# Second feed-forward: TensorE signals twice per pass, at a greater distance between up and down

## The reference

```python
x = x + jnp.tanh(g_ffn[1]) * _L1_ffn_ref(_layernorm(x, axis=-1), ...)

topk_idx, topk_weight = _gate(x, gate_w, e_bias)      # 4 of 16 experts for each row
g = jnp.einsum('th,eih->eti', x, gate_proj)           # 256 -> 128
u = jnp.einsum('th,eih->eti', x, up_proj)             # 256 -> 128
inter = jax.nn.silu(g) * u
expert_out = jnp.einsum('eti,ehi->eth', inter, down_proj)   # 128 -> 256
sel = expert_out[topk_idx, jnp.arange(T)[:, None]]
y = jnp.einsum('tkh,tk->th', sel, topk_weight)
shared_out = jax.nn.silu(sg) * su @ shared_down_w.T
return y + shared_out
```

## Time and profile before

| | |
|---|---|
| median of three runs | 1418.01 us (1416.52 to 1421.49) |
| span of the profiled execution, the only time of its own that the page gives | 1481.7 us |
| busy over the span: TensorE (matmul) | 1190.4 us, 80% |
| VectorE | 911.7 us, 62% |
| ScalarE | 784.9 us, 53% |
| GpSimd | 516.5 us, 35% |

### The profile page before, as it was taken

How to read it: one execution, slowest core, us unless ns; L and a number is a source line. 1 busy time by engine, 2 the same in 40 slices (tenths; PEclk the granted TensorE clock), 3 DMA queues, 4 the chain that set the end, 5 groups by cost and what they waited for, 6 DMA issues and landing times. The chain is left out here.

```text
span 1481.7 us, 27979 instructions
## 1 busy us (share of the span) xinstructions
PE 1190.4 (80%) x9258; PEld 1081.2 (73%) x9258; DVE 911.7 (62%) x2119; ACT 784.9 (53%) x2205; POOL 516.5 (35%) x585
## 2 busy tenths in 40 slices
PE   2776249997899999999999999975898767778674
PEld 1555139887799998888888888875887766667563
DVE  3887645552666666678657787766876322234667
ACT  2776115552566667665657665554654433345442
POOL 3566033553000001100354005543634555654442
PEclk9676559998999999999999999997999878889897
DMA  7753224553722000100233003443844545444896
GB/s 139 206 173 125 81 84 136 153 151 76 199 65 66 8 2 22 30 8 2 69 112 107 16 3 128 129 146 112 285 125 144 154 150 154 150 129 147 284 285 224
DMA packets 139588, 177.13 MB, mean 120 GB/s; under 512 B 22048, under 2 KB 120512, under 8 KB 139456
## 3 DMA queue, kind: packets, MB, share of 16 engines
q1 hardware_dynamic: 110752, 122.57, 28.8%
q0 software_dynamic: 17792, 43.14, 9.0%
q10 hardware_dynamic: 10912, 9.70, 1.9%
HBM read 107.28 MB, written 68.09 MB: 118 GB/s over the span
## 5 line engine op out<-in xcount | busy, mean ns | idle before, releaser
L1690 ACT ACTIVATE attend_s<-attend_s,attend_less 128x128 f32<-128x128 f32 x512 | 198.3, 392 | 108.4 <-DVE attend_less L1831 99.9
L2331 POOL DMA_INDIRECT answers<-ahead_plain,moe_dst x160 | 157.4, 984 | 186.5 <-ACT ahead_plain L2410 97.5
L1643 POOL TENSOR_TENSOR router_xn<-rest_acc,router_mv 128x512 f32<-128x512 f32 x12 | 12.7, 1058 | 426.6 <-DVE router_rs L1294 372.3
L81 PE MATMUL moe_psU<-moe_wh,moe_xl 128*128 (+1 forms) x384 | 118.1, 308 | 4.3 <-issue 3.3
L2477 DVE TENSOR_TENSOR moe_it<-moe_it,moe_psU 128x256 f32<-128x256 f32 x96 | 40.2, 418 | 128.9 <-ACT moe_it L2392 82.6
L83 PE MATMUL moe_psU<-moe_wh,moe_xh 128*128 (+1 forms) x384 | 115.9, 302 | 3.3 <-issue 3.2
L82 PE MATMUL moe_psU<-moe_wl,moe_xh 128*128 (+1 forms) x384 | 116.5, 303 | 2.3 <-issue 2.2
L1262 POOL DMA_INDIRECT slots<-router_row,router_idx x80 | 81.0, 1013 | 93.9 <-DMA router_row<-normed_rows 62.2
L1708 ACT ACTIVATE attend_pt<-attend_psS 128x1024 f32<-128x1024 f32 x64 | 65.5, 1024 | 83.2 <-PE attend_psS L1982 82.0
L1829 DVE SCALAR_TENSOR_TENSOR attend_s<-attend_psS,held_bias 128x1024 f32<-128x1024 f32 x64 | 78.0, 1219 | 44.3 <-PE attend_psS L1975 44.2
L2640 PE MATMUL moe_psI<-const_ident,moe_it 128*128 128x128 f32 x192 | 42.1, 305 | 78.4 <-DVE moe_il L2473 68.0
(11 more groups left out here) (384 smaller groups left out, 4175.6 us busy)
## 6 DMA issues: line engine op xcount, KB each, us to landing
ahead_plain<-slots SPq DMA_DIRECT2D x160, 129.0 KB
moe_both<-answers SPq DMA_DIRECT2D x28, 512.0 KB
router_row<-normed_rows SPq DMA_DIRECT2D x40, 256.0 KB
layer_raw<-in_wi_dram SPq DMA_DIRECT2D x8, 1024.0 KB, 4.8
layer_raw<-in_wo_dram SPq DMA_DIRECT2D x8, 1024.0 KB, 6.8
slots<-router_xn SPq DMA_DIRECT2D x4, 2048.0 KB, 11.0
ahead_plain<-in_gex_dram SPq DMA_DIRECT2D x17, 384.0 KB
moe_both<-normed_rows SPq DMA_DIRECT2D x24, 256.0 KB
```

The costliest lines, as they stand in the source:

```text
L81: pe.matmul(out, wl, mh, start=first, stop=False)
L1690: last = nc.scalar.activation(s[:, g, j, :], s[:, g, j, :], ACT.Exp, bias=less[:, g, j:j + 1], accum_out=sm[:, g, j:j + 1])
L2331: nc.gpsimd.indirect_dma_start(out=R.YT[q], out_offset=bass.IndirectOffsetOnAxis(ap=dst[:, r % NM, s:s + 1], axis=0), in_=yb[:, r % NY, s, ...
```

## The change

TensorE's four signals per pass become two. `upped` is raised by the last matmul of up(j), which now follows turn(j+2) and stands for both. `passed` is raised at the end of a pass, by turn_inner(j-2), which now follows down(j-4), and stands for both. All waits on the old four are put in terms of these. The table read stands at the end of the pass. There are 100 passes instead of 98, `it` has three buffers instead of two, the routing weights and targets twelve instead of eight, and the copy of the weights moves from ScalarE (`weighted`, removed with its semaphore) to VectorE's `targets`. The answers are asked for two passes later.

```diff
-    NT, NS, NM = 2, 4, 8
+    NT, NS, NM = 2, 4, 12
+    TURN_AHEAD, INNER_BEHIND, DOWN_BEHIND = 2, 2, 4
+    PASSES = PAIRS_ALL + DOWN_BEHIND
-        it = sb("it", [P, 2, 2, I1])
+        it = sb("it", [P, 3, 2, I1])
+        def pass_over(eng, j):
+            eng.wait_ge(passed, j - INNER_BEHIND + 1)
+        def turn_done(eng, j):
+            eng.wait_ge(upped, j + 1)
+        def up_done(eng, j):
+            eng.wait_ge(upped, j + TURN_AHEAD + 1)
+        def inner_done(eng, j):
+            pass_over(eng, j + INNER_BEHIND)
+        def down_done(eng, j):
+            pass_over(eng, j + DOWN_BEHIND)
-        answered_from = STARTS_OF[1] + NX + 4
+        answered_from = STARTS_OF[1] + NX + 4 + DOWN_BEHIND - 2
@@ SyncE, load
-                    sp.wait_ge(t_done, j - NX + 1)
+                    turn_done(sp, j - NX)
                     if not is_shared(j - NX):
                         sp.wait_ge(d_up, NTH[j - NX] + 1)
-                        sp.wait_ge(g_up, NTH[j - NX] + 1)
@@ ScalarE
-            for j in range(PAIRS_ALL + 2):
+            for j in range(PASSES):
+                if j + TURN_AHEAD < PAIRS_ALL:
+                    x_high(j + TURN_AHEAD)
                 if j < PAIRS_ALL:
                     silu(j)
-                if j + 2 < PAIRS_ALL:
-                    x_high(j + 2)
-                    if not is_shared(j + 2):
-                        weighted(j + 2)
-                if 1 <= j <= PAIRS_ALL:
-                    i_high(j - 1)
-                if j >= 2 and not is_shared(j - 2):
-                    y_out(j - 2)
+                if 0 <= j - INNER_BEHIND < PAIRS_ALL:
+                    i_high(j - INNER_BEHIND)
+                if j >= DOWN_BEHIND and not is_shared(j - DOWN_BEHIND):
+                    y_out(j - DOWN_BEHIND)
@@ VectorE, targets
+                v.tensor_copy(wd[:, r % NM, :], xg[:, j % NX, :, D])
@@ VectorE (its loop: x_low(j+2), inner(j), i_low(j-2), targets(j+2), add(j-4))
@@ TensorE
-            for j in range(PAIRS_ALL + 2):
+            for j in range(PASSES):
+                if j + TURN_AHEAD < PAIRS_ALL:
+                    last = turn(j + TURN_AHEAD)
                 if j < PAIRS_ALL:
-                    up(j, bases[j])
+                    last = up(j, bases[j])
+                    last.then_inc(upped, 1)
+                if j >= DOWN_BEHIND:
+                    last = down(j - DOWN_BEHIND, bases.pop(j - DOWN_BEHIND))
+                if 0 <= j - INNER_BEHIND < PAIRS_ALL:
+                    last = turn_inner(j - INNER_BEHIND)
+                if j >= INNER_BEHIND:
+                    last.then_inc(passed, 1)
                 if j + 1 in STARTS_OF:
                     pe.wait_ge(table_up, KIND[j + 1] + 1)
                 if j + 1 < PAIRS_ALL:
                     bases[j + 1] = bases_of(j + 1)
-                if j + 2 < PAIRS_ALL:
-                    turn(j + 2)
-                if 1 <= j <= PAIRS_ALL:
-                    turn_inner(j - 1)
-                if j >= 2:
-                    down(j - 2, bases.pop(j - 2))
```

More of the change, by code:

```diff
@@ L2382, in x_high @@
             def x_high(j):
-                act.wait_ge(t_done, j + 1)
+                turn_done(act, j)
                 nc.scalar.activation(xh[:, j % 2, :], psX[j % 2][:], ACT.Copy).then_inc(x_hi, 1)
             def i_high(j):
-                act.wait_ge(i_done, j + 1)
+                inner_done(act, j)
                 nc.scalar.activation(ih[:, j % 2], psI[:, 0:N], ACT.Copy).then_inc(i_hi, 1)
             def silu(j):
[L2391 to L2400, removed]
+                up_done(act, j)
+                nc.scalar.activation(it[:, j % 3], psU[j % 2][:].rearrange("p (s n) -> p s n", s=2)[:, :, 0:I1], ACT.Silu).then_inc(s_up, 1)
             def y_out(j):
                 r = NTH[j]
-                act.wait_ge(y_done, j + 1)
-                act.wait_ge(g_up, r + 1)
+                down_done(act, j)
+                act.wait_ge(d_up, r + 1)
                 if r >= NY:
@@ L2476, in inner @@
                 dve.wait_ge(s_up, j + 1)
[L2477 removed]
+                v.tensor_tensor(it[:, j % 3], it[:, j % 3], psU[j % 2][:].rearrange("p (s n) -> p s n", s=2)[:, :, I1:2 * I1], ALU.mult).then_inc(i_up, 1)
             def add(j):
[L2481 removed]
+                down_done(dve, j)
                 a = rows(acc[:, 2 * NTH[j]:2 * NTH[j] + 2, :])
@@ L2555, in _ @@
             R.aggregate(dve, LAST, stat3)
-            for j in range(PAIRS_ALL + 2):
+            for j in range(PASSES):
+                if j + TURN_AHEAD < PAIRS_ALL:
+                    x_low(j + TURN_AHEAD)
                 if j < PAIRS_ALL:
                     inner(j)
-                if j + 2 < PAIRS_ALL:
-                    x_low(j + 2)
-                if 1 <= j <= PAIRS_ALL:
[L2562 to L2566, removed]
+                if 0 <= j - INNER_BEHIND < PAIRS_ALL:
+                    i_low(j - INNER_BEHIND)
+                if j + TURN_AHEAD < PAIRS_ALL and not is_shared(j + TURN_AHEAD):
+                    targets(j + TURN_AHEAD)
+                if j >= DOWN_BEHIND and is_shared(j - DOWN_BEHIND):
+                    add(j - DOWN_BEHIND)
                 for k in (2 * j + 1, 2 * j + 2):
@@ L2609, in turn @@
                         last = nc.tensor.transpose(psX[j % 2][:, k * N + s * P:k * N + (s + 1) * P], xg[:, j % NX, s, k * P:(k + 1) * P], C["ident"][:])
-                last.then_inc(t_done, 1)
+                return last
             def bases_of(j):
@@ L2632, in up @@
                                        [part(w, bases[s], k * 2 * I1, 2 * I1) for w in (wh, wl)], k == 0, k == KD - 1)
-                last.then_inc(u_done, 1)
+                return last
             def turn_inner(j):
@@ L2639, in turn_inner @@
                 for s in range(2):
-                    last = nc.tensor.transpose(psI[:, s * P:(s + 1) * P], it[:, j % 2, s, :], C["ident"][:])
-                last.then_inc(i_done, 1)
+                    last = nc.tensor.transpose(psI[:, s * P:(s + 1) * P], it[:, j % 3, s, :], C["ident"][:])
+                return last
             def down(j, bases):
@@ L2650, in down @@
                                    [part(w, bases[s], 4 * I1, D) for w in (wh, wl)], True, True)
-                last.then_inc(y_done, 1)
+                return last
             split(pe, 0)
-            turn(0)
-            turn(1)
+            turn(0).then_inc(upped, 1)
+            turn(1).then_inc(upped, 1)
             bases = {0: bases_of(0)}
-            for j in range(PAIRS_ALL + 2):
+            for j in range(PASSES):
                 if j == STARTS_OF[0]:
```

8 lines of the change are left out of this document (4 added, 4 removed).

## The result

The changed kernel takes 1431.07 us (median of four runs, 1428.84 to 1432.39), the kernel before 1418.59 beside it (four runs). The ratio is 1.0081, 95% interval 1.0056 to 1.0106: slower by 12.5 us. The forecast was 1424.6, slower, with a range of its own of 1419 to 1430.

What follows compares the result with a forecast made beforehand. No engine was taken as full; TensorE's 2.79 us was the floor of a pass. 5.6 - 0.4 + 0.8 + 0.6 = +6.6 us on 1418.0 gave 1424.6 us; own range 1419 to 1430, whole range 1390 to 1431.

Steps and rivals of the forecast that it cites:

- The reading of the trace: TensorE signals arriving late in the second feed-forward belong to the profiled execution, explaining its 63.7 us over the timed runs.
- The rebuilt stage: Second feed-forward re-estimated without late signals, stretch by stretch: 380 us instead of the profiled 452.8.
- Signals at no cost: TensorE, each pass: two signals instead of four change nothing in a clean pass, taken as 0.
- the coarser waits: Engines waiting on the two remaining TensorE signals: x_high, y_out and i_high lose nothing in a clean pass.
- No slack from depth: TensorE's turn_inner wait on i_low: psI keeps one buffer, psU two, so clean passes get no faster, gain 0.
- Two more passes, counted once, +5.6: Late in the kernel: answers, combines and last y_out come two passes later, 2 x 2.79 us on the chain.
- Tail of VectorE +0.8: Last part: two more adds and one i_low queue behind the first combine, between 0 and 1.9 us.
- credit -0.4: i_low of the last routed pair no longer stands behind the last combine, saving 0.4 us.
- Weight copy +0.6 in passes 12 to 28: Copy moved to VectorE costs where VectorE is near its limit, 0 to 2.6 us, taken as 0.6.
- Wider target buffers at nothing: Twelve buffers for weights and targets only match the greater distance, with no gain counted.
- Rival B: Before turn(68): sends two passes later delay the second sort table, a stall of about 5 us, 1429.6 us; chance 0.12.

Runs made afterwards that it cites:

- the second trace: The kernel before, unchanged, run and profiled again: 1417.8 us, with a span of 1415.6 us.
- the near kernel: The changed kernel with turn_inner one pass behind up and down two, as in the kernel before, 98 passes: 1424.52 us, ratio 1.0038.
- far: The changed kernel with its sends put back to the pass they had in the kernel before: 1420.49 us, ratio 1.0014.
- four signals far: The kernel before's order and four signals at the changed kernel's distances, sends in their old pass, twelve targets, three inner buffers: 1420.81 us, ratio 1.0010.

## Why the prediction came out as it did

The measured 1431.07 us is slower, as forecast, but above the forecast's own range and at the upper end of the whole one. The direction is partly luck: the term that made the forecast slower, two passes of run-out on the chain, is hardly in the time, and what made the kernel slower is the lateness of the sends, which the forecast had as a rival at 0.12.

**The reading of the trace** was right: the late signals were of the profiled execution. The rebuilt stage, 380 us, was near the 387.8 of the second trace, but its terms missed in both directions and cancelled: 51 for passes 12 to 28 is 57.0, 115 for passes 29 to 57 is 103.4, 54 for 58 to 76 is 66.7. I had GpSimd's 3.97 us per pair as the length of a pass. That is GpSimd's pace (125.2 us for the 32 pairs with a send, 3.9 each), but GpSimd falls behind and passes 29 to 57 take 3.57 each. The backlog is paid where something waits for it: the odd pairs' rows and, last, `ready(1)`.

**Signals at no cost**: right for their number, by the changed kernel with two unused signals and by the one with four signals at the greater distance. That the coarser waits cost nothing is shown at the greater distance alone; the near kernel is 0.38% slower than before, and they may be part of that.

**No slack from depth**: as far as the times tell right (with the sends in the same pass, near 1.0038 and far 1.0014, before and four signals far 0.9993 and 1.0010), though the sign that I named for the contrary, a shorter wait on i_low, did appear (46.3 to 22.9 us). A wait can halve on an engine that isn't the bound.

**Two more passes, counted once, +5.6**: wrong in size. The last window does grow by 5.7 us and the combines start two passes later. But passes 68 to 76 are 4.9 us shorter, 3.8 of them in pass 76 (6.50 and 2.71), which the combines no longer hold up; from up(68) to the end before takes 138.0 us and the changed kernel 138.7. Of the chain, the stretch between the first and the last of the 24 combines stays (84 and 83 us), as I said; its start moved only 1.7 us against up(68) (24.0 and 25.7). Ahead of the first four combines VectorE waited 3.02, 0, 2.20 and 1.69 us before, and 0, 1.14, 0.50 and 1.62 in the changed kernel: the first of the later combines finds its data there.

**Tail of VectorE +0.8, credit -0.4**: on the chain, from the combine ahead of the last y_out to the end, it is 31.1 us before (from 1384.5) and 31.4 after (from 1398.5), +0.3 for a predicted +0.4. That it fits so well is partly chance: the two adds on the chain are 1.32 us where I had 0.8, and the load of the last answers is 0.4 us shorter (7.42 and 7.82). The chain of the changed kernel:

```profile
1400.59 0.84 ACT ahead_plain L2419 x2
...
1409.66 7.42 DMA ahead_plain<-answers
...
1420.24 1.32 DVE rest_acc L2491 x2
```

**Weight copy +0.6 in passes 12 to 28**: those are 1.4 us shorter, not longer, and passes 0 to 11 1.6 longer, both within the scatter of the traces; the copy is 205 ns, not 152. No cost shows. **Wider target buffers at nothing**: wrong. Eight buffers cost the kernel before with early sends 0.3%, some 4 us (0.9940 against 0.9970; the intervals just touch), where I had put 0. Whether the changed kernel, with its late sends, gains as much from them isn't shown.

**Rival B**, a stall of about 5 us before turn(68), given 0.12, has the right cause, late sends. I wrote that the old order was just on time and two passes more would show as a stall; the measured one is 7.43 us, 5.7 more than before, and with the 4.68 ahead of turn(61) passes 58 to 67 lose 7.1. The step that failed in my weighing is the backlog: I gave four pairs (15.9 us) as a mere possibility, and in the second trace of before 14.6 us lie between the end of y_out(57) and its scatter. For send and load I had some 3 us; they are 6.2. I missed the waits ahead of the odd pairs' loads, and put the price on top of the 5.6 that isn't there. B's 1429.6 is closer to the 1431.07 than the forecast, but these errors offset each other in it, so that is partly luck.

An account of the 12.5 us, by differences of ratios: sends two passes late, 0.67% (9.5 us, the changed kernel against the same with its sends moved back); greater distance and two signals with sends and targets the same, 0.40% (5.7 us, 0.9980 against 0.9940); twelve targets, -0.30% (-4.3 us). That is 10.9, against 11.5 by the ratio of 1.0081, with some 4 us of doubt in each part. It is not the only one, for the parts don't simply add. Taken the other way, the late sends cost 0.27% in the kernel before, and all the rest of the change 0.54% on top of them (1.0027 to 1.0081, 7.7 us); with the sends in their old pass the rest costs 0.1% (1.0014), with early sends 0.1% too (0.9970 to 0.9980), neither clear of noise. So the loss is that of late sends together with the rest of the change, and sends two passes earlier take most of it away. The parts of the twelve targets and of the greater distance come from kernels with early sends. Where the 0.40% lies is not settled: in the two traces (386.3 and 382.2 us) it is 2.4 us behind up(68) and about 1 us each in three earlier stretches, which single traces don't hold apart.

## What to carry to other kernels

When a change moves an item by some passes, look for what is tied to that item by count rather than by time. Here the sends rode on scatters, and moving one index back took 0.67% of the 0.81% off, with the changed pipeline as it was. A queue that falls behind costs at every point that waits for one of its items, so list these points, in the queues of other engines too, work out the backlog at each and compare it with the margin; and before a trace with unexplained releasers is taken as the base, profile the kernel once more.

## What the runs showed that I had not expected

The profiled execution of the kernel before was 66 us longer than a second one of the same kernel (1481.7 and 1415.6 us), with nothing different in the thirteen other traces. The Trainium skill, NOTIFIC: the notification-queue block, section on overflow, says that the recorder can hold its producers back; no row of these traces shows it, and the number of signals does not bring it on (two of the other four-signal kernels have spans of 1430.7 and 1420.4, next to their medians).

From the end of the last send to the turn that waits for it is 6.1 to 6.5 us in all nine kernels in which that turn waits (the send's landing, SyncE's wait and load, the load's landing), and 7.8 to 18.7 us in the four with earlier sends: a quick test of whether the send is what binds.
